# Loading each layer's weights and context one layer sooner, norming BiDAF's first batch on VectorE, and one-hots in two buffers

## What is computed

```
x = x + causal_attention(norm(x))                      # 16 heads, rotary
x = x + cross_attention(norm(x), ctx, ctx)             # ctx: 16 x 120 x 256
x = x + peer_ffn(norm(x))                              # product keys, top 10 of 8 heads
x = x + band_attention(norm(x))                        # bias on a band of the scores
x = x + bidaf(norm(x), ctx)                            # attention flow, W_l is 1024 -> 256
x = x + moe(norm(x))                                   # 8 experts, top 2
```

## Time and profile before

| | us |
|---|---|
| median of 3 runs (3757.82 to 3762.19) | 3761.95 |
| the profiled execution | 3762.07 |
| its span, first to last instruction | 3760.3 |
| stages, from the barrier ahead of each: causal, cross, peer | 0, 514.3, 910.5 |
| band, BiDAF, MoE | 2494.4, 2940.8, 3202.6 |

### The profile page before, as it was taken

How to read it: one execution, slowest core, us unless ns; L and a number is a source line. 1 busy time by engine, 2 the same in 40 slices (tenths; PEclk the granted TensorE clock), 3 DMA queues, 4 the chain that set the end, 5 groups by cost and what they waited for, 6 DMA issues and landing times. The chain is left out here.

```text
span 3760.3 us, 93455 instructions
## 1 busy us (share of the span) xinstructions
PE 3271.3 (87%) x33694; PEld 2778.2 (74%) x33695; DVE 2726.7 (73%) x10805; ACT 1199.3 (32%) x3136; POOL 2150.9 (57%) x2456
## 2 busy tenths in 40 slices
PE   6999957876599999999999999978888799799998
PEld 4777735554488888888888888855555577699998
DVE  6666634544999999999999999948888467433333
ACT  1443425543222222222222222216665222122221
POOL 4444325551577777777777777768887233233333
PEclk9999978998799999999999999989999789799999
DMA  5444434443000000000000000024453231566665
GB/s 154 112 106 110 110 83 111 123 113 131 1 2 2 2 2 2 2 2 2 2 2 2 2 2 2 2 70 124 122 127 99 70 106 52 141 181 182 181 181 134
DMA packets 256260, 277.91 MB, mean 74 GB/s; under 512 B 44145, under 2 KB 200817, under 8 KB 255345
## 3 DMA queue, kind: packets, MB, share of 16 engines
q1 hardware_dynamic: 242225, 253.69, 23.5%
q0 software_dynamic: 13632, 18.91, 3.5%
HBM read 187.63 MB, written 72.29 MB: 69 GB/s over the span
## 5 line engine op out<-in xcount | busy, mean ns | idle before, releaser
L1190 POOL TENSOR_TENSOR peer_hot_v<-peer_hot_e,peer_parts 80x512 bf16<-80x512 bf16 x768 | 991.1, 1317 | 321.2 <-DVE peer_hot_e L1233 311.6
L1009 PE MATMUL peer_ps_u<-peer_up,peer_g 128*128 128x256 f32 x2048 | 533.5, 407 | 0.6 <-DVE x_all L1331 0.6
L990 PEld LDWEIGHTS peer_ps_h<-peer_xnT,peer_down 128*128 128x128 f32 x4096 | 513.4, 197 | 16.0 <-DMA peer_down<-in_peer_down 1.2
L990 PE MATMUL peer_ps_h<-peer_xnT,peer_down 128*128 128x128 f32 x4096 | 512.9, 280 | 1.0 <-DMA peer_down<-in_peer_down 1.0
L1000 PE MATMUL peer_ps_w<-peer_hot_v,peer_hot_u 80*128 80x32 bf16 x12288 | 347.3, 177 | 145.3 <-DVE peer_g L1245 98.6
L1000 PEld LDWEIGHTS peer_ps_w<-peer_hot_v,peer_hot_u 80*128 80x128 bf16 x12288 | 337.1, 97 | 167.4 <-issue 90.9
L1009 PEld LDWEIGHTS peer_ps_u<-peer_up,peer_g 128*128 128x128 f32 x2048 | 392.6, 201 | 53.2 <-issue 1.0
L1087 ACT ACTIVATE peer_g<-peer_ps_h 128x512 f32<-128x512 f32 x256 | 152.9, 597 | 842.3 <-PE peer_ps_h L990 842.0
L1237 DVE TENSOR_TENSOR peer_hot_u<-peer_count,peer_uvT 80x2048 bf16<-80x2048 bf16 x256 | 349.4, 1365 | 0.0
L2160 POOL DMA_INDIRECT out<-moe_y,moe_target x71 | 112.6, 1585 | 312.5 <-DVE moe_y L2261 309.6
L2104 PE MATMUL moe_ps_t<-moe_xgT,moe_w 128*128 128x128 f32 x2272 | 267.4, 276 | 0.0
(11 more groups left out here) (370 smaller groups left out, 7107.8 us busy)
## 6 DMA issues: line engine op xcount, KB each, us to landing
moe_w<-in_moe_w SPq DMA_DIRECT2D x142, 512.0 KB, 4.5
causal_qs<-causal_qscratch SPq DMA_DIRECT2D x32, 384.0 KB, 4.0
cross_qs<-cross_qscratch SPq DMA_DIRECT2D x32, 384.0 KB, 3.6
band_qs<-band_qscratch SPq DMA_DIRECT2D x32, 384.0 KB, 4.0
route_w<-in_moe_w SPq DMA_DIRECT2D x8, 1024.0 KB, 5.9
causal_qscratch<-causal_part SPq DMA_DIRECT2D x32, 192.0 KB, 2.6
causal_kscratch<-causal_part SPq DMA_DIRECT2D x32, 192.0 KB, 2.0
causal_ks<-causal_kscratch SPq DMA_DIRECT2D x32, 192.0 KB, 4.3
```

The lines of the kernel that those rows point to most:

```text
L990: mm = nc.tensor.matmul(ps_h[:, n % 2, k * P:(k + 1) * P], down[:, c, 4 * n + k, :], xnT[:, par, c, :], start=(c == 0), stop=(c == DC - 1))
L1009: mm = nc.tensor.matmul(ps_u[:], g[:, par, v, :], up[:, v, :], start=(v == 0), stop=(v == EV - 1))
L1190: ins = nc.gpsimd.tensor_tensor(hot_v[0:SEL, n % RING, part], hot_e[0:SEL, n % RING], w, ALU.mult)
```

## The change

- A `Room` called Ahead lives through the whole kernel. It holds wq and wk (for cross and later band), pack, spread and peer's wq. pack and spread are loaded once, in the causal stage. Cross's wq and wk are loaded in the causal stage, at moments(2); peer's wq in the cross stage, at moments(2); band's wq and wk in the peer stage, behind up.
- Context holds ctx through causal and cross. It is loaded in the causal stage in four pieces, at moments(4) to moments(7). The copy into ctx_one is gone: PE transposes out of ctx_sb.
- Last holds BiDAF's wl through the rest; it is loaded in the band stage, at moments(2).
- BiDAF: DVE norms batch 0 itself, ahead of its wait for loads; SP fetches the first two contexts first; PE waits for loads only where it first needs them (`row` of batch 0); from h = 2 on the expert's load stands ahead of the stores.
- MoE: the one-hots have two buffers in turn, and the names are multiplied in place.
- Ahead, Context and Last are Rooms of their own, with a close of their own: Context's behind the cross stage, the other two at the end.

```
+class Ahead:
...
+    def __init__(self, nc, ctx):
+        r = Room(nc, ctx, "ahead")
+        self.w = {n: r.sb(n, [P, DC, D]) for n in ("wq", "wk")}
+        self.pack = r.sb("pack", [P, SLOT])
+        self.spread = r.sb("spread", [P, DC, P])
+        self.peer_wq = r.sb("peer_wq", [P, DC, 2 * 8 * 32])
+        self.cross_in = r.sem("cross_in")
+        self.peer_in = r.sem("peer_in")
+        self.band_in = r.sem("band_in")
...
+    def weights(self, sp, d, kind, sem):
+        for n in self.w:
+            sp.dma_start(self.w[n][:], self.chunks(d[f"{kind}_{n}"])).then_inc(sem, 16)
...
+    def during_causal(self, sp, d, b):
+        if b == 2:
+            self.weights(sp, d, "cross", self.cross_in)
+
+    def during_cross(self, sp, d, b):
+        if b == 2:
+            sp.dma_start(self.peer_wq[:], self.chunks(d["peer_wq"])).then_inc(self.peer_in, 16)
+
+
+class Context:
...
+    def __init__(self, nc, ctx, name):
+        r = Room(nc, ctx, name)
+        self.ctx = r.sb("ctx", [P, B, D])
+        self.ctx_in = r.sem("ctx_in")
...
+    def during(self, sp, d, b):
+        if 4 <= b < 4 + self.PIECES:
+            n = B // self.PIECES
+            some = slice((b - 4) * n, (b - 3) * n)
+            sp.dma_start(self.ctx[0:CTX, some, :], d["ctx"].rearrange("b k c -> k b c")[:, some, :]).then_inc(self.ctx_in, 16)
...
+class Last:
+
+    def __init__(self, nc, ctx, name):
...
+        self.wl = r.sb("wl", [P, 8, D])
+        self.wl_in = r.sem("wl_in")
...
+    def during(self, sp, d, b):
+        if b == 2:
+            sp.dma_start(self.wl[:], d["bidaf_wl"].rearrange("(c p) n -> p c n", p=P)).then_inc(self.wl_in, 16)
...
+        pack, spread = ahead.pack, ahead.spread
+        if rope:
+            w = {n: sb(n, [P, DC, D]) for n in names}
+            w["wo"] = sb("wo", [P, DC, D])
+        else:
+            w = {n: sb(n, [P, DC, D]) for n in ("wv", "wo")}
+        own = list(w)
+        nload = len(own) + (2 if rope else 0)
+        if not rope:
+            w |= ahead.w
...
-            ctx_one = sb("ctx_one", [P, D])
+            ctx_sb = context.ctx
...
-            for n in w:
+            for n in own:
                 sp.dma_start(w[n][:], chunks(d[f"{kind}_{n}"])).then_inc(weights, 16)
-            sp.dma_start(pack[:], d["pack"]).then_inc(weights, 16)
-            sp.dma_start(spread[:], d["spread"]).then_inc(weights, 16)
             if rope:
+                sp.dma_start(pack[:], d["pack"]).then_inc(weights, 16)
+                sp.dma_start(spread[:], d["spread"]).then_inc(weights, 16)
...
-            if cross:
-                sp.dma_start(ctx_sb[0:CTX, :, :], d["ctx"].rearrange("b k c -> k b c")).then_inc(weights, 16)
...
+                def moments(self, b):
+                    if rope:
+                        ahead.during_causal(sp, d, b)
+                    if not cross:
+                        context.during(sp, d, b)
+                    if cross:
+                        ahead.during_cross(sp, d, b)
...
+            if cross:
+                pe.wait_ge(ahead.cross_in, ahead.CROSS)
+                pe.wait_ge(context.ctx_in, context.ALL)
+            if kind == "band":
+                pe.wait_ge(ahead.band_in, ahead.BAND)
...
-                            mm = nc.tensor.transpose(ps_p[:, 1, c * CTX:(c + 1) * CTX], ctx_one[0:CTX, c * P:(c + 1) * P],
+                            mm = nc.tensor.transpose(ps_p[:, 1, c * CTX:(c + 1) * CTX], ctx_sb[0:CTX, b, c * P:(c + 1) * P],
...
-                    if cross:
-                        ins = nc.vector.tensor_copy(ctx_one[0:CTX, :], ctx_sb[0:CTX, b, :])
...
-        wq = sb("wq", [P, DC, 2 * NQ * HALF])
+        wq = ahead.peer_wq
...
-            sp.dma_start(wq[:], d["peer_wq"].rearrange("(c p) n -> p c n", p=P)).then_inc(loaded, 16)
...
+            ahead.weights(sp, d, "band", ahead.band_in)
...
+            pe.wait_ge(ahead.peer_in, ahead.PEER)
...
-            sp.dma_start(wl[:], d["bidaf_wl"].rearrange("(c p) n -> p c n", p=P)).then_inc(loaded, 16)
...
-                sp.wait_ge(loaded, 16 * NLOAD)
...
+            for z in streams:
+                fetch(z, 0, z.k)
+            sp.dma_start(bl[:], d["bidaf_bl"].partition_broadcast(P)).then_inc(loaded, 16)
+            sp.dma_start(vec[:], d["bidaf_vec"]).then_inc(loaded, 16)
+            sp.dma_start(b3[:], d["bidaf_b"]).then_inc(loaded, 16)
+
             for h in range(B + 4):
-                if h < B:
-                    fetch(streams[h % NS], h // NS, h)
                 if h == 1:
                     weights()
+                if NS <= h < B:
+                    fetch(streams[h % NS], h // NS, h)
+                if 2 <= h < 2 + E:
+                    sp.dma_start(route.w2[:, h - 2], w2_in[:, h - 2]).then_inc(route.weights, 16)
                 if 0 <= h - 2 < B:
                     store(streams[h % NS], (h - 2) // NS, h - 2)
                 if 0 <= h - 3 < B:
                     store_rows(streams[(h - 3) % NS], (h - 3) // NS, h - 3)
-                if 2 <= h < 2 + E:
-                    sp.dma_start(route.w2[:, h - 2], w2_in[:, h - 2]).then_inc(route.weights, 16)
...
-            pe.wait_ge(loaded, 16 * NLOAD)
-            pe.wait_ge(ready, 1)
...
+                if b == 0:
+                    pe.wait_ge(loaded, 16 * NLOAD)
+                    pe.wait_ge(ready, 1)
+                    pe.wait_ge(last.wl_in, 16)
...
-                if b == 0:
-                    pool.wait_ge(ready, 1)
+                if b == 1:
+                    pool.wait_ge(streams[0].c_ready, 1)
...
-            norm(streams[0], 0, 0)
...
+            for t in range(TT):
+                ins = nc.vector.tensor_scalar(first.c[:, t, :], x_all[:, t, :], mean[:, t, :], rstd[:, t, :], ALU.subtract, ALU.mult)
+            ins.then_inc(first.c_ready, 1)
+            dve.wait_ge(first.c_ready, 1)
+            dve.wait_ge(last.wl_in, 16)
...
+        rowhot = sb("rowhot", [P, 2, FEW, P, TOPE], F16)
+        tilehot = sb("tilehot", [P, 2, FEW, JT, TOPE], F16)
...
-                        mm = nc.tensor.matmul(ps_y[:, 0, 0:JT], rowhot[:, t, :, k], tilename[:, t, :, k],
+                        mm = nc.tensor.matmul(ps_y[:, 0, 0:JT], rowhot[:, n % 2, t % FEW, :, k], tilehot[:, n % 2, t % FEW, :, k],
...
+                mm.then_inc(hot_used, 1)
...
+                wait(dve, hot_used, n - 1)
+                steps.link(nc.vector.tensor_tensor(tilehot[:, n % 2], iota2[:, 0:JT, :].unsqueeze(1).broadcast_to((P, FEW, JT, TOPE)),
+                                                   tileb[:, few, :].unsqueeze(2).broadcast_to((P, FEW, JT, TOPE)), ALU.is_equal))
+                nc.vector.tensor_tensor(rowhot[:, n % 2], iota2[:].unsqueeze(1).broadcast_to((P, FEW, P, TOPE)),
                                         rowb[:, few, :].unsqueeze(2).broadcast_to((P, FEW, P, TOPE)), ALU.is_equal)
-                nc.vector.tensor_tensor(tilename[:, few], tilehot[:, few],
+                nc.vector.tensor_tensor(tilehot[:, n % 2], tilehot[:, n % 2],
                                         name[:, few, :].unsqueeze(2).broadcast_to((P, FEW, JT, TOPE)), ALU.mult).then_inc(hot_ready, 1)
...
+            dve.wait_ge(hot_used, NHOT)
...
+        ahead = Ahead(nc, ctx)
+        with ExitStack() as early:
+            context = Context(nc, early, "early")
+            attention_stage(nc, "causal", stats, ident, d, ahead, context)
+            attention_stage(nc, "cross", stats, ident, d, ahead, context)
+        peer_stage(nc, stats, ident, d, ahead)
+        last = Last(nc, ctx, "last")
+        attention_stage(nc, "band", stats, ident, d, ahead, last)
         route = Route(nc, ctx.enter_context(ExitStack()))
-        bidaf_stage(nc, stats, ident, d, route)
+        bidaf_stage(nc, stats, ident, d, route, last)
```

More of the change, by code:

```diff
@@ L117, in vector, with chunks, attention_stage @@
         steps.link(v.tensor_tensor(self.rstd[:], self.guess[:], self.t0[:], ALU.mult))
-def attention_stage(nc, kind, stats, ident, d):
+class Ahead:
[8 more added lines that the diff above has]
+        self.band_in = r.sem("band_in")
+    def chunks(self, ap):
+        return ap.rearrange("(c p) n -> p c n", p=P)
+    def weights(self, sp, d, kind, sem):
+        for n in self.w:
+            sp.dma_start(self.w[n][:], self.chunks(d[f"{kind}_{n}"])).then_inc(sem, 16)
+    CROSS, PEER, BAND = 16 * 2, 16, 16 * 2
+    def during_causal(self, sp, d, b):
[9 more added lines that the diff above has]
+        self.ctx_in = r.sem("ctx_in")
+    PIECES = 4
+    ALL = 16 * PIECES
+    def during(self, sp, d, b):
[5 more added lines that the diff above has]
+    def __init__(self, nc, ctx, name):
+        r = Room(nc, ctx, name)
+        self.wl = r.sb("wl", [P, 8, D])
[3 more added lines that the diff above has]
+            sp.dma_start(self.wl[:], d["bidaf_wl"].rearrange("(c p) n -> p c n", p=P)).then_inc(self.wl_in, 16)
+def attention_stage(nc, kind, stats, ident, d, ahead, context):
     x_all, mean, rstd = stats.x_all, stats.mean, stats.rstd
@@ L837, with peer_stage @@
```

(23 more changed lines are left out.)

14 lines of the change are left out of this document (1 added, 13 removed).

## The result

The changed kernel takes 3729.69 us (median of 6 runs, 3723.55 to 3739.13), the kernel before 3761.82 beside it; the ratio is 0.9912, 95% interval 0.99 to 0.9925, so 33 us less (28 to 38). Forecast were 15.6 us less.

A forecast was written before the change was run, and what follows sets the result against it. Stages run one behind the other, with waits for loads at their starts and SP's loop of issues and landings pacing cross. Gains of 20.1 us less 4.5 lost made 15.6, so 3762.07 became 3746.5 us; range 3739 to 3754.

The forecast's parts named there:

- Into BiDAF: Term for BiDAF's start and SP's order inside: qT starts earlier, 4.2 us gained; reordered loads cost or gain 0.
- rival C: Early loads are paid where they are put: 28.2 us against 20.1 gained, 3770.2 us; chance 0.04 in full, 0.08 in part.
- Start of cross: Fewer loads at cross's start end DVE's wait for the context: 14.3 us gained, between 13.1 and 14.5.
- signs of being wrong: Causal longer by over 2 us, cross behind its start shorter by over 2, or a bias wait replacing the context's.
- Peer's start: Without wq ahead of it iota lands before rstd ends: the wait goes, 1.6 us gained, between 0.8 and 1.7.
- BiDAF's start: DVE norms batch 0 and wl is loaded earlier, so qT starts sooner: 4.2 us gained, between 2.7 and 4.5.
- Peer's wq in cross: Loading peer's wq in cross, where SP has no gap, costs 2.0 us, between 0.46 and 3.0.
- wl in band: Loading wl (1,024 KB) in band costs 1.0 us after SP's waits for POOL; bounds 0 and 4.1.
- Causal's loads: Cross's wq, wk and the context loaded in causal fit SP's 4.5 us gap: cost 0, upper bound 19.6.
- Copies: Dropping cross's 16 context copies on DVE, 4.6 us in all, gains 0; bounds 0 and 4.5.
- MoE: Two one-hot buffers and the multiply in place cost 0, or 0.3 us for semaphores.
- Closes: Three added closes, one between cross and peer, two at the end, cost 1.5 us; bounds 1.0 and 2.5.

The follow-up runs named there:

- experiment 7: Changed kernel with DVE's copy of each batch's context in cross kept as before: ratio 0.992 (0.9906 to 0.9934), cross 386.9 us.
- experiment 4: Changed kernel with only the fifth expert's load (h = 6) behind the stores again; single timed run, BiDAF stage 245.4 us.
- experiments 1 to 3 and 5: Kernel before, expert loads ahead of stores: 0.9945; changed kernel, that order undone: 0.9967; kernel before, loads behind BiDAF's loop: 0.999; changed kernel, context loaded at cross's start: 0.993.

## Why the prediction was wrong

**The step that failed** is the last sentence of "Into BiDAF": SP's new order "moves loads that PE doesn't wait for: 0". PE doesn't wait for the experts' loads, and yet their place on the queue cost it 18.8 us: the term looked at the load that is moved and not at the context issued right behind it, for which PE does wait. The view of which the earlier trace rows shows some lines had it, in one that I left out there:

```profile
bidaf_q<-in_ctx SPq DMA_DIRECT2D x16, 120.0 KB, 3.9
```

That is 3.9 us in the median, and up to 6.3 by the landings above, where a store of 90 KB takes 2.3. So what rival C says, that no row shows a small transfer held up behind a large one in mid-stage, is true of the rows printed and not of the trace. The steps had it too: 13.2 us in the last five, 14.7 to 17.6 in those with expert loads. And a stop costs more than itself, since the clock falls behind it. The order alone measures 21 us (15 to 26; 18.8 by the steps), and 12.4 (7.5 to 17) is what the change gives without it, against 15.6 forecast. No rival had this one. Nor were the other terms as good as that looks: measured one by one, below, they make 10.8 and not 15.6, which the interval can't tell apart.

**Start of cross**, 14.3 forecast, 13.5 measured: bo landed 0.88 us behind rstd, the case named in its lower bound, 13.1. So one of the prediction's own signs of being wrong did come, a wait for a bias, but at 0.88 us of the 14.19.

**Peer's start**, 1.6: the wait went, but only 0.6 is left at the first residual sum (165.5 us into the stage against 166.1), since PE's sixteen matmuls for the scores took 2.08 us at a granted clock of 0.50, where before they took 1.16 at 1.00. By the end nothing is left that could be told from the scatter of this stage (its last sum stands at 1581.9 to 1584.9 in the twelve traces).

**BiDAF's start**, 4.2: 4.3.

**Peer's wq in cross**, 2.0 against 3.6, above the bound of 3.0. **wl in band**, 1.0 against 2.8, within its bounds. (The estimate of 1.7 given beside the first is further off still; the fit of the Trainium skill that it uses is for DMAs issued from GpSimd, and SP issued this one.) In both I took the landing for the one thing that is late and set POOL's lead against it. The trace shows the load right ahead of the store of k's parts, whose landing is waited for next (5.84 instead of 2.10 us), where POOL's lead, which stands at another wait of the same queue, is no help. The Trainium skill ("DMA: Bandwidth & Descriptors", section "Two DMAs through the same engine are not ordered") says that within one queue of one DMA engine descriptors start in order, though they are pipelined. By that rule a small transfer starts behind the large one; the traces agree, 5.84 us against 2.10.

**Causal's loads**, 0: right; 28.5 us a batch in every trace. SP's timeline of the changed kernel, in causal, shows why the same store of k's parts isn't late here: the gap of 4.5 us stands between the load and that store, and the load that needs it comes 2.02 us behind it, as in before:

```profile
247.39 0.45 SPq L164 DMA_DIRECT2D early_ctx<-in_ctx  x1
251.11 0.36 SPq L470 DMA_DIRECT2D causal_kscratch<-causal_part  x1
253.13 0.31 SPq L481 DMA_DIRECT2D causal_qs<-causal_qscratch  x1
```

**Copies**, 0: not refuted, but open by up to 3 us (experiment 7). By the forecast cross was to take 2.0 us longer behind its first transpose, for peer's wq; to its barrier it took 375.4 where before it took 375.5, although that load costs 3.6. **MoE**, 0: right. To the first barrier of the end it takes 557.2 us in before and 556.5 in the changed kernel, with 556.3 to 558.0 in all twelve. **Closes**, 1.5: the barriers that the change adds stand 0.4 us behind the one ahead of them, so 1.2.

Rival C, the slower one, was right in its mechanism in the two stages where a load did meet a landing that SP waits for, and wrong in causal, which held 19.6 of its 28 us. Summed anew from what was measured: 13.5 + 0.6 + 4.3 + 18.8 - 3.6 - 2.8 - 1.2 = 29.6, against 33 (28 to 38) in the timed runs. The profiled pair has 33.8. The difference of 4.2 has 3 in BiDAF's warm-up and 3.7 in cross, for which no term here accounts (the copies, or scatter), less what causal and peer lost by scatter.

## What to carry to other kernels

Where a diff only reorders DMA issues on a queue, look at what is sent behind the big load, not only at who needs the big load itself. Compare the landing time of each small transfer with that of the same size elsewhere, and the steps of the batches with and without the load. An idle time of PE marked "issue" ahead of the same instruction in batch after batch was a wait without a name here; the landings, laid beside the starts, named it. Price it with the time that the clock stays down behind it. A load put into a busy queue was free where the queue then waited for an engine (causal), and cost 3 to 4 us where the next wait was for the landing of a transfer issued right behind it (cross and band).

## What was unexpected of the hardware

Each of the nine stops of PE from 0.82 to 1.98 us in BiDAF (four in before, four with the order undone, one with one late load) was followed by a granted clock of 0.5, for some 3 to 10 us, though PE was busy again behind it (3005 to 3010 in before: busy 5.00 of 5.00, clock 0.53); the stop of 0.35 us was not. The length of the fall doesn't follow that of the stop: 1.94 us was followed by 7 us of it, 1.14 us by 10. At BiDAF's start the full clock came 20 us in at the earliest (changed kernel) and 35 at the latest (experiment 4) behind the same instructions on PE; what decides it these runs don't show. The changed kernel's times scatter over 15.6 us in six runs (3723.55 to 3739.13). Those of the kernel before scatter over 7 us in the six beside them and over 15.5 in the seventeen beside experiments 1 to 3 and 5, so the one kernel isn't shown to scatter more than the other.
